# Head 3's attention probabilities through memory, with its scores and the products of heads 2 and 3 moved in TensorE's order

## The chip, the cores and the metric

One core of one Trainium2 chip. The metric is the device time of one execution in microseconds, the median of three runs. TensorE (PE) multiplies matrices, VectorE (DVE), ScalarE (ACT) and GpSimd (POOL) do elementwise work, and the sync engine (SP) issues nearly all the DMAs, in the order in which they are written. Each engine runs its instructions in order and waits on semaphores.

## The reference, cut to what matters

Tokens are 8 batches of 128, width 512. Two residual layers follow each other; the first one's attention is where the change lies: 32 heads of width 128, in 8 groups of 4.

```python
h_q = (rms(layernorm(x)) @ w_q.T)      # per head h
h_k, h_v = ctx @ w_k.T, ctx @ w_v.T
score = einsum('bqhd,bkhd->bhqk', h_q, h_k) + position_bias
score = where(mask, score, -inf); score = softmax(score, -1)
attn = einsum('bhqk,bkhd->bqhd', score, h_v)
x = x + tanh(g) * (hidden + attn @ w_out.T)
```

Behind it come a quantized feed-forward layer, a single-head attention and a layer of routed adapters, which the change does not touch.

## The kernel before, in words

The kernel is written out by hand: for each engine a list of calls, and the order of these lists is the order of the work. The groups of four heads are group 0 (`"first"`), groups 1 to 6 (`"loop"`, a loop on every engine) and group 7 (`"last"`). Float32 is split in a high and a low part; a product of two splits is three passes. In the loop the queries and keys of two heads come from seven products (`product`, Strassen's way, in the order `ORDER` = P1, P6, P2, P7, P5, P4, P3) whose right sides are blocks of x or of the context and combined blocks, fetched from memory into `ring` by SP (`fetch`, L407). Group 0 uses plain products (`plain`) and VectorE makes the combined blocks there (`combine_x`), which POOL splits (`combined_lo`) and SP stores (`put`, L404).

For each head, 8 batches at once:
- `scores` (TensorE, L1954) writes banks 4 and 5, four batches each. The second half waits until the head before has left bank 5.
- `softmax_in` (VectorE, L1374 and L1376) adds bias and mask (`bm`, made by POOL's `biasmask`, L682) and takes the maximum; `exps` (ScalarE, L952) does eight exponentials.
- `softmax_out` (VectorE), per half: a reciprocal (L1383), the multiplication into `turned_blocks` (L1396), and for heads 0 to 2 a transposition of 32x32 blocks (L1400).
- For heads 0 to 2 SP writes `turned_blocks` to memory (`passed`, L432) and reads it back so that whole blocks change places (`back`, four DMAs, L442) into `keyed`, the transposed probabilities. For head 3 (`h == TURNED`) VectorE writes them plainly (L1392), TensorE transposes them (`transposes`, L1982) and ScalarE copies them into `keyed` (`pt_out`, L939).
- `attend` (TensorE, L1970) multiplies values by `keyed` into banks 6 and 7; `ao_hi` (ScalarE, L958) and `ao_lo` (VectorE, L1405) split the result into `ao`.
- `project` (TensorE, L1998) makes 16 output tiles, 0 to 7 from heads 0 and 1 and 8 to 15 from heads 2 and 3, and `add_out` (VectorE, L1414) adds each to `acc`.

TensorE's order around the change, in a loop group: the seven products for heads 2 and 3 (the last is P3), scores of head 2, tiles 0 to 5, scores of head 3, tiles 6 and 7, two products, the product of head 2 with the values, three products, `transposes`, one product, head 3's product with the values, one product, tiles 8 to 15. SP's order there: write of head 2, a weight load (`v0`), return of head 2, a weight load (`q0`, L397), the bias (L446), then ring fetches and loads. In group 7 the products for the next group are replaced by `keys`, products of the second layer: their weights are loaded by SP into `raw_k`, scaled and split by ScalarE (`key_scaled`, L986, and `split_hi`, L998), which then copies two output weights (`vo_hi`, L906), all ahead of the exponentials of head 3. At the very start `warm` (L1841) runs matmuls on zeros.

Of the kernel before, what the change touches and what calls it, by code (L numbers as in the profile page):

```python
# [12 lines left out]
P = 128  # L13
# [79 lines left out]
def build(nc, a, out):  # L93
# [91 lines left out]

    TURNED = 3
# [64 lines left out]
    with ctx:  # L251
# [65 lines left out]

        s_pt, s_pte = s_cT, s_xT

# [72 lines left out]
        with nc.Block() as block:  # L392

            @block.sync
            def _(sp):
# [33 lines left out]
                def passed(g, h):  # L429

                    sp.wait_ge(s_turned, g * 2 * TURNED + 2 * h + 2)
# [3 lines left out]
                def back(g, m, h):  # L435
# [4 lines left out]
                    sp.wait_ge(s_passed, 16 * (g * TURNED + h) + 16)  # L440
# [47 lines left out]
                put(1, 3, 3)  # L488
                sp.wait_ge(s_bm, GH)
                bias_in(1)  # L490
                sp.wait_ge(s_plain, plain_at["q3b"])
# [14 lines left out]
                def body(g, m):  # L506
# [35 lines left out]
                    passed(g, 2)  # L542
                    sp.wait_ge(s_flo, 3 * prods(g, 3) + 3)
                    load(g + 1, "v0", 0)
                    back(g, m, 2)
# [3 lines left out]
                    bias_in(g + 1)  # L549
                    last_piece(prods(g, 3), 0)  # L550
# [10 lines left out]

                sp.wait_ge(s_prod, last_prod)
                sp.dma_start(raw_k[:, :, :], a["w_key"]).then_inc(s_raw["key"], 16)
                sp.wait_ge(s_spill, 32)
                sp.dma_start(raw_f[:, :, :], expanded).then_inc(s_raw["ffn"], 16)
                sp.dma_start(bkr[:, :], a["bk"].partition_broadcast(P)).then_inc(s_bk, 16)
                sp.dma_start(fnw[:, :], a["fnw"].partition_broadcast(P)).then_inc(s_fnw, 16)
                passed(LAST, 2)
                back(LAST, "last", 2)
                sp.wait_ge(s_vo_lo, vo_done(LAST, "last", "o3"))  # L570
                sp.dma_start(rows, a["rows"].partition_broadcast(P)).then_inc(s_rows, 16)
                sp.dma_start(wbm, a["w_bm"]).then_inc(s_bm1, 16)
                sp.wait_ge(s_tlo["key"], KC)
# [13 lines left out]
            def _(pool):  # L587
# [138 lines left out]
                combined_lo(1, 1, 3)  # L726
                vo_lo(0, "first", "o2")
                vo_lo(0, "first", "o3")
                plain_lo(9)
                biasmask(0, 3)  # L730
# [126 lines left out]
            def _(act):  # L857
# [75 lines left out]
                def pt_out(g):  # L933


                    act.wait_ge(s_pv, g * 2 * GH + 6)
                    for s in range(2):
                        act.wait_ge(s_pt, B + 2 * g + s + 1)
                        act.activation(keyed[:, :, :, :].rearrange("p i b q -> p (i b q)")[:, half(s)], bank[6 + s][:, :],  # L939
                                       ACT.Copy).then_inc(s_pte, 1)  # L940

# [128 lines left out]
                combined_hi(1, 2, 2, spare[:, :, :])  # L1070
                combined_hi(1, 3, 3)
# [13 lines left out]
                def body(g, m):  # L1085
# [38 lines left out]
                    if not last:  # L1124
                        first_out(g, m, 3)
                        vo_hi(g, "loop", "w0")
                        vo_hi(g, "loop", "w1")
# [1262 lines left out]
```

## Time and profile before

| What | us |
|---|---|
| median of 3 runs (lowest, highest) | 959.33 (958.12, 960.22) |
| the profiled execution | 959.01 |
| its span, first to last instruction | 957.2 |
| TensorE busy, matmuls | 941.9 (98%) |
| VectorE, ScalarE, POOL busy | 594.2, 399.5, 497.3 |
| mean rate of the DMAs | 208 GB/s |
| waits of TensorE for probabilities from memory | 5.6 |

How to read it: the groups take 97.4 us each (the first output tile of group 2 starts at 294.67, that of group 3 at 392.38), and the second layer starts near 821. Times of rows are microseconds from the start of the span, the mean of one instruction is in ns. The durations of matmuls overlap; their starts give the pace.

### The profile page before, as it was taken

Reading aid. Unit: us, or ns where it says so; the run is one execution under the profiler, and the core shown is the slowest. Engines: PE = TensorE matmul, PEld = TensorE weight load, DVE = VectorE, ACT = ScalarE, POOL = GpSimd, SP = SyncE. Lnnn points to the kernel's source line nnn. Section 1 sums busy time; section 2 is a strip of 40 time slices with the busy share of each in tenths; the row PEclk is TensorE's granted clock in tenths of the full one; section 3 lists DMA queues with packets and bytes.
Section 4 is the critical chain, followed back from the end, with each engine's and each line's share of the span. In section 5 each row is a group of like instructions: output and inputs, shape, how many; then the busy total and the mean of one; then the engine's idle time right before and its main releaser. Section 6 shows DMA issues by size and latency. Waiting matters only on the chain.

```text
span 957.2 us, 15391 instructions
## 1 busy us (share of the span) xinstructions
PE 941.9 (98%) x4850; PEld 793.9 (83%) x4850; DVE 594.2 (62%) x1020; ACT 399.5 (42%) x1080; POOL 497.3 (52%) x463
## 2 busy tenths in 40 slices
PE   9999899999999999999999999999999999999998
PEld 8888688788888888888888888888888888888885
DVE  4888846385538553855486447654666966756754
ACT  5765424252434233433443333433443346646630
POOL 3756754454446453646374637463646336687530
PEclk9999999999999999999999999999999999999999
DMA  7145676775687567766777667767687665200002
GB/s 283 45 152 222 234 255 249 259 266 196 241 276 275 219 241 263 271 244 241 251 271 256 241 241 260 270 248 237 226 292 266 230 224 183 91 23 1 2 1 88
DMA packets 67380, 199.44 MB, mean 208 GB/s; under 512 B 8720, under 2 KB 21264, under 8 KB 66320
## 3 DMA queue, kind: packets, MB, share of 16 engines
q1 hardware_dynamic: 66336, 197.67, 57.4%
q10 hardware_dynamic: 1008, 1.32, 0.4%
q8 instruction: 19, 0.31, 0.1%
q14 instruction: 17, 0.14, 0.0%
HBM read 174.85 MB, written 24.12 MB: 208 GB/s over the span
## 4 chain that ended last, share of the span: by engine, by line
PE 78%; DVE 8%; DMA 7%; issue 2%; SPq 2%; ACT 1%; POOL 1%; DVEq 0%; ACTq 0%
PE bank L1921 23%; PE bank L1998 16%; PE bank L2102 10%; PE bank L1937 10%; DMA keyed<-passing 6%; PE bank L1970 6%; PE bank L1954 5%; PE bank L1897 3%; PE bank L2126 2%; DVE turned_blocks L1396 1%; SPq L442 1%; DVE kt L1436 1%; DVE turned_blocks L1400 1%; PE bank L1982 1%; PE bank L2255 1%
## 5 line engine op out<-in xcount | busy, mean ns | idle before, releaser
L1998 PE MATMUL bank<-wvo,ao 128*128 128x512 f32 x768 | 179.9, 391 | 0.7 <-issue 0.6
L1937 PE MATMUL bank<-wvo,ct 128*128 128x512 f32 x768 | 177.7, 390 | 0.0
L1998 PEld LDWEIGHTS bank<-wvo,ao 128*128 128x128 f32 x768 | 143.0, 188 | 30.1 <-issue 1.0
L1937 PEld LDWEIGHTS bank<-wvo,ct 128*128 128x128 f32 x768 | 143.5, 188 | 29.3
L603 POOL TENSOR_TENSOR wvo<-stage,wvo 128x512 fp32r<-128x512 f32 x64 | 85.4, 1357 | 148.4 <-ACT wvo L906 148.3
L1921 PE MATMUL bank<-ring,wkq 128*128 128x512 f32 x648 | 157.4, 390 | 0.0
L1921 PEld LDWEIGHTS bank<-ring,wkq 128*128 128x128 f32 x648 | 121.2, 188 | 25.1
L1414 DVE SCALAR_TENSOR_TENSOR acc<-bank,gated_rows,acc 128x512 f32<-128x512 f32 x128 | 93.2, 742 | 39.4 <-PE bank L1998 38.3
L952 ACT ACTIVATE bank<-bank,nmax 128x128 f32<-128x128 f32 x256 | 88.2, 351 | 55.6 <-DVE nmax L1376 55.6
L1405 DVE TENSOR_TENSOR ao<-bank,ao 128x512 fp32r<-128x512 f32 x64 | 43.9, 691 | 106.6 <-ACT ao L958 106.6
L1436 DVE TENSOR_TENSOR qt<-bank,qt 128x512 f32<-128x512 f32 x98 | 66.4, 690 | 57.4 <-PE bank L1921 56.0
L682 POOL TENSOR_TENSOR bm<-maskneg,bias 128x1024 f32<-128x1024 f32 x32 | 78.9, 2465 | 26.0 <-DVE bank L1374 26.0
L945 ACT ACTIVATE vals<-bank 128x512 f32<-128x512 f32 x64 | 38.4, 600 | 94.7 <-PE bank L1937 94.4
L623 POOL TENSOR_TENSOR wkq_raw<-stage 128x256 f32<-128x256 f32 x27 | 20.3, 754 | 110.7 <-PE bank L1921 102.2
L1436 DVE TENSOR_TENSOR kt<-bank,kt 128x512 f32<-128x512 f32 x91 | 60.4, 682 | 26.6 <-PE bank L1921 25.0
L958 ACT ACTIVATE ao<-bank 128x512 fp32r<-128x512 f32 x64 | 37.9, 599 | 80.7 <-PE bank L1970 79.0
L1970 PEld LDWEIGHTS bank<-keyed,vals 128*128 128x128 f32 x512 | 61.0, 191 | 12.7 <-DMA keyed<-passing 11.1
L1970 PE MATMUL bank<-keyed,vals 128*128 128x128 f32 x512 | 63.6, 277 | 5.7 <-DMA keyed<-passing 5.6
L1374 DVE TENSOR_TENSOR bank<-bank,bm 128x512 f32<-128x512 f32 x64 | 44.4, 694 | 37.3 <-PE bank L1954 36.4
L1921 PE MATMUL bank<-xb,wkq 128*128 128x512 f32 x252 | 65.5, 395 | 0.0
L649 POOL TENSOR_TENSOR wkq<-wkq_raw,wkq 128x1024 fp32r<-128x1024 f32 x27 | 65.2, 2414 | 0.0
L1954 PEld LDWEIGHTS bank<-kt,qt 128*128 128x128 f32 x512 | 62.1, 191 | 3.4 <-DVE turned_blocks L1396 0.9
(187 smaller groups left out, 1511.9 us busy)
## 6 DMA issues: line engine op xcount, KB each, us to landing
ring<-combined SPq DMA_DIRECT2D x216, 512.0 KB, 6.3
stage<-in_w SPq DMA_DIRECT2D x63, 512.0 KB, 4.2
passing<-turned_blocks SPq DMA_DIRECT2D x24, 512.0 KB, 2.9
keyed<-passing SPq DMA_DIRECT2D x96, 128.0 KB, 3.2
combined<-work SPq DMA_DIRECT2D x16, 512.0 KB, 3.6
xraw<-in_x SPq DMA_DIRECT2D x2, 1024.0 KB, 11.3
bias<-in_bias SPq DMA_DIRECT2D x8, 256.0 KB, 4.5
cs<-in_ctx SPq DMA_DIRECT2D x1, 2048.0 KB, 7.8
```

The source lines that it names most:

```text
L603: pool.tensor_tensor(wvo[:, 1, h, :], stage[:, vo_stage(g, m, c)[0], :], wvo[:, 0, h, :].bitcast(fp32), ALU.subtract).then_inc(s_vo_lo, 1)
L649: pool.tensor_tensor(wkq[:, 3:7, 1, :, :].rearrange("p k c d -> p k (c d)"), wkq_raw[:, 3:7, 1, :, :].rearrange("p k c d -> p k (c d)"), w ...
L682: pool.tensor_tensor(bm[:, :, :], maskneg[:, :, :], bias[:, h:h + 1, :].to_broadcast([P, B, P]), ALU.add).then_inc(s_bm, 1)
L952: act.activation(scores, scores, ACT.Exp, bias=nmax[:, b:b + 1], accum_out=esum[:, b:b + 1]).then_inc(s_exp, 1)
L1414: dve.scalar_tensor_tensor(out=acc[:, b, :], in0=bank[un_of[m][f"o{i}"] % RING if to is None else to][:, :], scalar=gated_rows[:, b:b + 1] ...
L1436: dve.tensor_tensor(dst, bank[un_of[m][f"{ADDED[step]}.{j}"] % RING][:, :], other, ALU.add).then_inc(s_add, 1)
L1921: mm = pe.matmul(bank[b][:, :], wkq[:, FACTOR[p], w, c, :], right(s), start=(c == 0 and w + s == 0), stop=(c == 1 and w == 1))
L1937: mm = pe.matmul(bank[un_of[m][u] % RING][:, :], ct[:, i, c, b * P:(b + 1) * P], wvo[:, j, c, :], start=(c == 0 and i + j == 0), stop=(c = ...
L1954: mm = pe.matmul(bank[4 + s][:, (b - 4 * s) * P:(b - 4 * s + 1) * P], qt[:, h % 2, b * P:(b + 1) * P], kt[:, h % 2, b * P:(b + 1) * P], st ...
L1970: mm = pe.matmul(bank[6 + s][:, (b - 4 * s) * P:(b - 4 * s + 1) * P], vals[:, b, h * P:(h + 1) * P], right, start=True, stop=True)
L1998: mm = pe.matmul(bank[to][:, :], ao[:, h, p, b * P:(b + 1) * P], wvo[:, j, 2 * pair + h, :], start=(h == 0 and p + j == 0), stop=(h == 1 a ...
L2102: mm = pe.matmul(bank[b][:, 0:n], left(i, c), right[:, j, c, :], start=(c == 0 and i + j == 0), stop=(c == KC - 1 and i == 1 and last))
```

## The change

Head 3 takes the way of heads 0 to 2: `TURNED`, `transposes` and `pt_out` are gone, `softmax_out` turns blocks for every head, and `passed` and `back` are called for head 3. On TensorE the scores of head 3 stand behind three output tiles (before: six), the product of head 2 directly behind tile 7 and that of head 3 three products later (in group 7: one and two `keys` are moved). VectorE's, ScalarE's, POOL's and SP's lists follow: `softmax_in` and `softmax_out` of head 3 move forward between the additions; in SP's list the return of head 2 moves ahead of the `v0` load, the write of head 3 behind that load, and its return behind the `q0` load and the bias; in group 7 the write of head 2 moves ahead of the key weights' load. The diff, with context lines left out:

```diff
@@ -182,8 +182,6 @@
-    TURNED = 3
     R_FFN, R_BQ, R_BASE = range(3)
@@ -314,9 +312,6 @@
-        s_pt, s_pte = s_cT, s_xT
@@ -428,7 +423,7 @@
-        sp.wait_ge(s_turned, g * 2 * TURNED + 2 * h + 2)
+        sp.wait_ge(s_turned, g * 2 * GH + 2 * h + 2)
         sp.dma_start(passing[h % 2, :, :, :, :].rearrange("i k j c -> (i k) j c"),
@@ -437,7 +432,7 @@
             sp.wait_ge(s_pv, g * 2 * GH + 2 * h)
-        sp.wait_ge(s_passed, 16 * (g * TURNED + h) + 16)
+        sp.wait_ge(s_passed, 16 * (g * GH + h) + 16)
         for j in range(4):
@@ -485,9 +480,11 @@
     put(1, 2, 2)
-    put(1, 3, 3)
     sp.wait_ge(s_bm, GH)
     bias_in(1)
+    passed(0, 3)
+    put(1, 3, 3)
+    back(0, "first", 3)
     sp.wait_ge(s_plain, plain_at["q3b"])
@@ -540,13 +537,15 @@
         passed(g, 2)
+        back(g, m, 2)
         sp.wait_ge(s_flo, 3 * prods(g, 3) + 3)
         load(g + 1, "v0", 0)
-        back(g, m, 2)
+        passed(g, 3)
         sp.wait_ge(s_vo_lo, vo_done(g, "loop", "o3"))
         bias_in(g + 1)
+        back(g, m, 3)
         last_piece(prods(g, 3), 0)
@@ -559,17 +558,19 @@
+    passed(LAST, 2)
     sp.wait_ge(s_prod, last_prod)
     sp.dma_start(raw_k[:, :, :], a["w_key"]).then_inc(s_raw["key"], 16)
+    back(LAST, "last", 2)
     sp.wait_ge(s_spill, 32)
     sp.dma_start(bkr[:, :], a["bk"].partition_broadcast(P)).then_inc(s_bk, 16)
+    passed(LAST, 3)
     sp.dma_start(fnw[:, :], a["fnw"].partition_broadcast(P)).then_inc(s_fnw, 16)
-    passed(LAST, 2)
-    back(LAST, "last", 2)
     sp.wait_ge(s_vo_lo, vo_done(LAST, "last", "o3"))
     sp.dma_start(wbm, a["w_bm"]).then_inc(s_bm1, 16)
+    back(LAST, "last", 3)
     sp.wait_ge(s_tlo["key"], KC)
@@ -724,10 +725,10 @@
     combined_lo(1, 1, 3)
+    biasmask(0, 3)
     vo_lo(0, "first", "o2")
     plain_lo(9)
-    biasmask(0, 3)
@@ -929,15 +930,6 @@
-    def pt_out(g):
-        act.wait_ge(s_pv, g * 2 * GH + 6)
-        for s in range(2):
-            act.wait_ge(s_pt, B + 2 * g + s + 1)
-            act.activation(keyed[:, :, :, :].rearrange("p i b q -> p (i b q)")[:, half(s)], bank[6 + s][:, :],
-                           ACT.Copy).then_inc(s_pte, 1)
@@ -1068,14 +1060,13 @@
     combined_hi(1, 2, 2, spare[:, :, :])
+    exps(0, 3, range(2))
     combined_hi(1, 3, 3)
-    exps(0, 3, range(2))
     vo_hi(0, "first", "w0")
     plain_out("k4b")
-    pt_out(0)
     plain_out("k5a")
@@ -1121,15 +1112,14 @@
         exps(g, 3, range(2))
+        ao_hi(g, 2)
         if not last:
             vo_hi(g, "loop", "w1")
-        ao_hi(g, 2)
         if last:
                 split_hi("ffn", c)
-        pt_out(g)
         ao_hi(g, 3)
@@ -1381,18 +1371,10 @@
         dve.reciprocal(rinv[:, bs], esum[:, bs]).then_inc(s_rinv, 1)
-        if h and s == 0:
-            dve.wait_ge(s_passed, 16 * (g * TURNED + h))
-        elif s == 0 and m != "first":
-            dve.wait_ge(s_pt, B + 2 * g)
+        if s == 0 and (m, h) != ("first", 0):
+            dve.wait_ge(s_passed, 16 * (g * GH + h))
         dve.wait_ge(s_rinv, n + 1)
-        if h == TURNED:
-            dve.tensor_tensor(turned_blocks[:, :, :, :].rearrange("p j b k -> p (j b k)")[:, half(s)].rearrange("p (b k) -> p b k", b=4),
-                              bank[4 + s][:, :].rearrange("p (b k) -> p b k", b=4),
-                              rinv[:, bs].unsqueeze(2).to_broadcast([P, 4, P]), ALU.mult).then_inc(s_p, 1)
-            return
         dve.tensor_tensor(turned_blocks[:, :, bs, :].rearrange("p j b k -> p b j k"),
@@ -1657,17 +1639,17 @@
     softmax_out(0, "first", 2, 1)
+    softmax_in(0, 3)
     add_out(0, "first", 3)
     add_out(0, "first", 4)
+    softmax_out(0, "first", 3, 0)
+    add_out(0, "first", 5)
     combine_x([8])
-    add_out(0, "first", 5)
+    softmax_out(0, "first", 3, 1)
+    add_out(0, "first", 6)
     combine_x([9])
-    softmax_in(0, 3)
-    add_out(0, "first", 6)
     add_out(0, "first", 7)
-    softmax_out(0, "first", 3, 0)
-    softmax_out(0, "first", 3, 1)
     ao_lo(0, 2)
@@ -1703,28 +1685,26 @@
         add_out(g, m, 1)
+        softmax_out(g, m, 2, 1)
         add_out(g, m, 2)
-        softmax_out(g, m, 2, 1)
+        softmax_in(g, 3)
         add_out(g, m, 3)
+        softmax_out(g, m, 3, 0)
         add_out(g, m, 4)
+        softmax_out(g, m, 3, 1)
         add_out(g, m, 5)
-        softmax_in(g, 3)
         add_out(g, m, 6)
         add_out(g, m, 7)
-        softmax_out(g, m, 3, 0)
-        softmax_out(g, m, 3, 1)
+        ao_lo(g, 2)
         if last:
             key(0)
-            ao_lo(g, 2)
             key(1)
+            ao_lo(g, 3)
             key(2)
+        else:
+            sums(g, m, 3, ("u2", "C11"))
             ao_lo(g, 3)
-        else:
-            sums(g, m, 3, ("u2",))
-            ao_lo(g, 2)
-            sums(g, m, 3, ("C11", "u3", "C22", "u4", "C21"))
-            ao_lo(g, 3)
-            sums(g, m, 3, ("C12",))
+            sums(g, m, 3, ("u3", "C22", "u4", "C21", "C12"))
             for i in range(B, 2 * B):
@@ -1956,32 +1936,15 @@
     def attend(g, h):
-        if h < TURNED:
-            pe.wait_ge(s_keyed, 64 * (g * TURNED + h) + 64)
+        pe.wait_ge(s_keyed, 64 * (g * GH + h) + 64)
         for s in range(2):
                 pe.wait_ge(s_val_out, 8 * g + 4 * s + 4)
-            if h == TURNED:
-                pe.wait_ge(s_pte, B + 2 * g + s + 1)
-            else:
-                pe.wait_ge(s_aolo, g * 2 * GH + 2 * h + s + 1)
+            pe.wait_ge(s_aolo, g * 2 * GH + 2 * h + s + 1)
             for b in range(4 * s, 4 * s + 4):
-                right = keyed[:, :, b, :] if h < TURNED else keyed[:, :, :, :].rearrange("p i b q -> p (i b q)")[:, b * P:b * P + P]
                 mm = pe.matmul(bank[6 + s][:, (b - 4 * s) * P:(b - 4 * s + 1) * P],
-                               vals[:, b, h * P:(h + 1) * P], right, start=True, stop=True)
+                               vals[:, b, h * P:(h + 1) * P], keyed[:, :, b, :], start=True, stop=True)
             mm.then_inc(s_pv, 1)
-    def transposes(g):
-        n = g * 2 * GH + 2 * TURNED
-        for s in range(2):
-            pe.wait_ge(s_p, n + s + 1)
-            pe.wait_ge(s_aolo, n + s + 1)
-            for b in range(4 * s, 4 * s + 4):
-                mm = pe.transpose(bank[6 + s][:, (b - 4 * s) * P:(b - 4 * s + 1) * P],
-                                  turned_blocks[:, :, :, :].rearrange("p j b k -> p (j b k)")[:, b * P:b * P + P], ident[:, :])
-            mm.then_inc(s_pt, 1)
@@ -2030,15 +1993,14 @@
     scores(0, "first", 2)
-    for i in range(6):
+    for i in range(3):
         project(0, "first", i)
     scores(0, "first", 3)
-    project(0, "first", 6)
-    project(0, "first", 7)
+    for i in range(3, B):
+        project(0, "first", i)
     plain("k4a")
     plain("k4b")
-    transposes(0)
     plain("k5a")
@@ -2068,30 +2030,25 @@
         scores(g, m, 2)
-        for i in range(6):
+        for i in range(3):
             project(g, m, i)
         scores(g, m, 3)
-        project(g, m, 6)
-        project(g, m, 7)
+        for i in range(3, B):
+            project(g, m, i)
+        attend(g, 2)
         if last:
             keys(0)
-            attend(g, 2)
             keys(1)
-            transposes(g)
+            attend(g, 3)
             keys(2)
-            attend(g, 3)
             for i in range(B, 2 * B):
             return
-        product(g, m, 3, "P1")
-        product(g, m, 3, "P6")
-        attend(g, 2)
-        for p in ORDER[2:5]:
+        for p in ORDER[:3]:
             product(g, m, 3, p)
-        transposes(g)
-        product(g, m, 3, "P4")
         attend(g, 3)
-        product(g, m, 3, "P3")
+        for p in ORDER[3:]:
+            product(g, m, 3, p)
         for i in range(B, 2 * B):
```

## Rows read from the trace of the kernel before

**Rows 1.** The page, busy time, share of the span and instructions of TensorE
```profile
PE 941.9 (98%) x4850; PEld 793.9 (83%) x4850; DVE 594.2 (62%) x1020; ACT 399.5 (42%) x1080; POOL 497.3 (52%) x463
```

**Rows 2.** Groups by line, TensorE; busy us, mean ns, then idle before
```profile
L1982 PE MATMUL bank<-ident,turned_blocks 128*128 128x128 f32 x64 | 8.5, 274 | 2.3 <-DVE ao L1405 2.3
```

**Rows 3.** The chain that ended last, group 2; start us, us, what
```profile
294.67 8.20 PE bank L1998 x36
302.87 1.78 PE bank L1954 x16
...
310.10 1.78 PE bank L1970 x16
...
316.03 0.87 PE bank L1982 x8
...
318.28 1.78 PE bank L1970 x16
...
321.46 10.88 PE bank L1998 x48
```

**Rows 4.** Timeline of VectorE, group 2; start us, us, what
```profile
298.84 1.37 DVE L1414 SCALAR_TENSOR_TENSOR acc<-bank,gated_rows,acc 128x512 f32<-128x512 f32 x2
300.13 0.17 DVE L1383 RECIPROCAL rinv<-esum 128x4 f32<-128x4 f32 x1
...
301.05 0.71 DVE L1400 STREAM_TRANSPOSE turned_blocks<-turned_blocks 128x512 f32<-128x512 f32 x1
...
303.86 0.70 DVE L1374 TENSOR_TENSOR bank<-bank,bm 128x512 f32<-128x512 f32 x1
...
306.53 1.64 DVE L1414 SCALAR_TENSOR_TENSOR acc<-bank,gated_rows,acc 128x512 f32<-128x512 f32 x2
```

**Rows 5.** Timeline of ScalarE, group 2, the last exponential of head 3
```profile
307.74 0.37 ACT L952 ACTIVATE bank<-bank,nmax 128x128 f32<-128x128 f32 x1
```

**Rows 6.** Timeline of SP's queue, group 2; start and time of the issues
```profile
301.79 0.32 SPq L432 DMA_DIRECT2D passing<-turned_blocks  x1
...
304.65 1.74 SPq L442 DMA_DIRECT2D keyed<-passing  x4
306.65 0.36 SPq L397 DMA_DIRECT2D stage<-in_w  x1
307.30 0.36 SPq L446 DMA_DIRECT2D bias<-in_bias  x1
```

**Rows 7.** Waits of TensorE in the whole run; us, times, longest
```profile
PE bank L1970 <- DMA keyed<-passing: 5.6, 9, 1.7
```

**Rows 8.** The chain that ended last, head 0's return in group 2
```profile
271.02 8.41 DMA keyed<-passing
```

**Rows 9.** Timeline of SP's queue, group 0
```profile
101.63 0.32 SPq L432 DMA_DIRECT2D passing<-turned_blocks  x1
...
111.15 3.19 SPq L404 DMA_DIRECT2D combined<-work  x4
```

**Rows 10.** Timeline of TensorE, group 0, the product of head 2
```profile
108.69 2.05 PE L1970 MATMUL bank<-keyed,vals 128*128 128x128 f32 x16 [1.14 <-DMA keyed<-passing]
```

**Rows 11.** The chain that ended last, output tile 8 of group 0
```profile
124.34 10.88 PE bank L1998 x48
```

**Rows 12.** The DMA view, the load of the key weights; us to landing last
```profile
raw_k<-in_w_key SPq DMA_DIRECT2D x1, 1024.0 KB, 4.8
```

**Rows 13.** Timeline of ScalarE, group 7
```profile
787.46 2.59 ACT L986 ACTIVATE raw_k<-raw_k,fncol 128x512 f32<-128x512 f32 x4
...
792.00 1.17 ACT L906 ACTIVATE wvo<-stage 128x512 fp32r<-128x512 f32 x2
```

**Rows 14.** The chain that ended last, output tiles of group 7
```profile
784.03 8.20 PE bank L1998 x36
...
810.25 11.18 PE bank L1998 x48
```

**Rows 15.** Timeline of TensorE at the start, matmuls on zeros
```profile
1.05 4.44 PE L1841 MATMUL bank<-qt 128*128 128x128 f32 x20 [1.05 <-DVE qt L1306]
```

## The prediction

> **What bounds the kernel now.** Read the page first. TensorE is busy for 941.9 of 957.2 us [rows 1], so what the change does is decided by what TensorE executes and by what it waits for. The profiled execution took 959.01 us, 1.8 us more than its span and 0.3 us under the median 959.33; every sum below is made against 959.0. The second view is the chain of waits in one group of heads (group 2; groups 1 and 3 to 6 repeat it): from the end of head 2's scores at 294.67 to output tile 8 at 321.46 it is TensorE without a gap [rows 3]. I call 294.67 zero: output tiles cost 1.37 each (8.20 for 6), a head's scores or its product with the values 1.78, a product of seven 1.37 as well, the eight transposes 0.87, and tile 8 begins at 26.8. The third is what feeds it: VectorE's and ScalarE's softmax [rows 4, 5] and SP's queue [rows 6]. The waits list says that heads 0 to 2, which already go through memory, are late nine times, 5.6 us in all [rows 7]: that trip has almost no slack.
>
> **What is removed.** `transposes` (64 matmuls) and `pt_out` go. The group view gives them 274 ns each [rows 2], but they overlap: in the chain eight take 0.87 [rows 3], so 7.0 us in eight groups, plus the 2.3 us wait of group 0 [rows 2]. The Trainium skill, "TensorE: Matmul & The Clock Gate", Part 4: PE-mode transpose, gives about 275 ns for a transpose in a kernel; by that eight would be worth 2.2 us and the whole removal 17.6. The chain's spacing decides, and I take 7.0. `pt_out`'s two copies on ScalarE hide beside TensorE, and their going gives nothing.
>
> **What is added, in a loop group.** First VectorE. Now it ends head 2's second half at 301.05 + 0.71, that is +7.1 [rows 4]. One addition (0.65, half of 1.29) moves behind it, so it ends at +6.45, and `passed` for head 2 is issued then. The scores of head 3 come three tiles after zero, at +4.1. Their first half (0.89) ends at +5.0, but the second needs bank 5, freed by the multiplication that ends at +5.75: TensorE waits 0.75. This isn't added to the sum, because a later wait covers it. Next VectorE adds tile 2 (+7.1) and does `softmax_in(3)`: 306.53 - 303.86 = 2.67, to +9.75. POOL's `biasmask` needs only head 2's scores read and keeps its place, so it is in time. Tile 3 is added (+10.4). The exponentials end 308.11 - 303.86 = 4.25 after `softmax_in` began [rows 4, 5], at +11.35, so they cost nothing. Then two `softmax_out` of 1.63 each (300.13 to 301.76) with one addition between: head 3's turned probabilities are ready at **+14.3**.
>
> Now the trip through memory. SP is free (head 2's return was issued near +9.3, the load of v0 after it). For head 2 now the write is issued at 301.79, the returns from 304.65, and the product starts at 310.10 without a wait: at most 8.3 us [rows 6, 3]. In group 0, with no load between write and return, the product waited for it and began at 108.69 after the issue at 101.63: 7.06 us [rows 9, 10]. For head 3 the q load (512 KB) and the bias (256 KB), which now stand behind head 2's return [rows 6], fall between write and return. Head 2's trip carries one load of 512 KB there; I take its 8.3 plus 0.5 for the other 256 KB: 8.8. Ends: 7.06, and, if the queues are as full as behind head 0, 2.9 for the write, 1.3 to the last issue and 8.41 after it [rows 6, 8] = 12.6. So head 3's product starts at **+23.1**. TensorE's own work brings it there at 8 x 1.37 + 1.78 + 0.75 + 1.78 + 3 x 1.37 = +19.4 (a little later if head 2's return is late), so it waits near 3.7 us. Behind the product (2.05 when it was waited for [rows 10]) come four products, 5.5: tile 8 at +30.65 against +26.8. That is **3.8 us slower** per group. In six groups 22.8; waits for head 2 that this absorbs are part of the 5.6 us [rows 7], and I give a third back, 1.8: **+21.0**. The ring fetches behind `back` 3 go out at about +19; the first to be used, for P4, is wanted at +28. Next group's weights need the last products, whose distance to the next group is unchanged. Both cost nothing while a landing stays under 9 us.
>
> **Group 0.** Here VectorE also makes the combined blocks. `softmax_in(3)` (2.67) and both `softmax_out` (3.3) move ahead of step 9 of `combine_x`, so POOL's lower part, and with it the stores that SP issued at 111.15 [rows 9], come about 6 us later, 117.1. In SP's queue `passed` for head 3 stands behind one such store and the bias: some 1.5 later, 118.6. Another 1 MB store stands between it and the return. The trip is 9.2 by my choice (7.06 to 12.6): product at 127.8, then 2.05 and one unit of 2.73: tile 8 at 132.6 against 124.34 [rows 11]: **+8.3**, with the transposes' waits already inside.
>
> **Group 7.** `passed` for head 2 moves ahead of the 1 MB key weights in SP's queue. They are issued now before 784.03; then near 784.03 + 6.45 + 0.4 = 790.9. The landing takes 4.8 [rows 12] and one more for the write before it: 796.7. On ScalarE the scaling and splitting of these weights and two weight copies, 793.17 - 787.46 = 5.7 [rows 13], stand ahead of head 3's exponentials, so these start at 802.4 and end at 805.2 (eight in 2.8). The second `softmax_out`, behind an addition, ends at 807.8. SP then issues head 3's write, and rows, norm weights and adapters (1.3 MB) lie between it and the return: trip 9.6, product at 817.4. With keys(2), 2.77, tile 8 comes at 822.2 against 810.25 [rows 14]: **+12.0**.
>
> **The clock.** The granted clock is 1.00 (2.4 GHz) in every stretch, and no wait behind the first scores exceeds 2.3 us. At the start 20 matmuls took 4.44 us, 0.22 each [rows 15], where the transposes take 0.11 [rows 3]: half the pace, as at 1.2 GHz, though the column doesn't show it. What a wait of 6 to 9 us does, this trace doesn't show: at least 0, at most that start again, 2.2 lost each time. Groups 0 and 7 get three such waits, 0 to 6.6; I take two, **4.4**, because the one idle engine that the trace shows, at the start, was slow. The same page of the Trainium skill, Part 1: The HAM clock gate, says that an idle TensorE is set to half its clock; by that rule all three would cost.
>
> **Sum**: 959.0 + 21.0 + 8.3 + 12.0 + 4.4 = 1004.7, so 1005. With trips of 7.06 everywhere and no clock loss: 6 x 1.74 + 2.1 + 2.5 less, 985. With 12.6 everywhere and 6.6 of clock: 22.8 + 3.4 + 3.0 + 2.2 more, 1036.
>
> **Rivals.** (a) The trips are short, as in group 0: 985 to 993. For it, the v0 load no longer stands inside head 2's trip; against, the bias and q loads do inside head 3's. (b) The queues are fuller than for head 2: from 1020 to 1036. For it, head 0's return took 8.41 after its last issue [rows 8]; against, eight ring fetches stood ahead of that one, and here only three transfers. (c) TensorE falls to half its clock after the loop's waits of 3.7 us too: six more times 2.2, that is 1018. For it, they are longer than the 2.3 seen; against, the products on both sides are dense. (d) **Faster.** The return lands before TensorE asks: this needs a trip under 19.4 - 14.3 = 5.1 us in the loop. Then 7.0 are gained and, with the late returns and the 2.3, up to 9 more goes: 950. Against it is the shortest trip seen, 7.06, two microseconds above the point. (e) In group 7 the order of the key weights' load doesn't hold up head 3, since they land early enough: then that group costs 3.8 and the sum is 996. Against, ScalarE runs its instructions in order.
>
> **Numbers.** Chances: forecast (993 to 1013) 0.55, (a) 0.15, (b) 0.12, (c) 0.07, (d) 0.03, (e) 0.08. The range 985 to 1022 holds forecast, (a), (c), (e) and the near end of (b), and leaves out (d) and most of (b). About 0.2%, 2 us, is what a measurement of this kernel can tell from no change. Faster only in (d): 0.03; same 0.01; slower 0.96.
>
> **What would show it.** In the profile after: waits of TensorE's line of the head products for the return from memory, some 3.7 us in each of six groups and more in groups 0 and 7, some 40 us in all; the write of head 3 issued 14.3 after the end of head 2's scores; a wait of 0.75 in the scores of head 3; key weights issued near 6.9 after that zero in group 7 instead of before it; the matmul after a long wait at twice its spacing. The forecast is wrong if the product of head 3 starts within 19.4 of zero, or if VectorE is ready much before 14.3.

## The result, and the profile after

The changed kernel takes 1018.55 us (median of 4 runs, 1016.99 to 1022.18), the kernel before, run beside it, 958.73 (957.88 to 960.22): a ratio of 1.0621, 95% interval 1.0599 to 1.0644. It is 60 us slower (59.8 by the medians, 59.5 by the ratio). The forecast was 1005 with a range of 985 to 1022: sign and range hold, the size was 13.5 too small. The profiled execution took 1017.53, its span is 1015.7, 58.5 more than before.

The page of the kernel after: busy time, and the granted clock in 40 slices (tenths).

```profile
PE 954.0 (94%) x4786; PEld 801.2 (79%) x4786; DVE 601.1 (59%) x1036; ACT 390.5 (38%) x1064; POOL 494.8 (49%) x463
PEclk9999989999999999999999999999989997999999
```

TensorE has 64 instructions fewer and is busy 12.1 us **longer** than in [rows 1]. Work was taken away and the time of the rest grew: mostly matmuls at a lower clock, as the windows below show. The other 46 us are idle time. The waits of TensorE (total, times, longest):

```profile
PE bank L1945 <- DMA keyed<-passing: 41.1, 17, 9.5
PE bank L1934 <- DVE turned_blocks L1378: 10.7, 9, 3.2
PE bank L2059 <- DVE acc L1396: 3.6, 1, 3.6
```

L1945 is `attend`, L1934 `scores`, L1961 `project`, L2059 the second layer's `keys` (L1970, L1954 and L1998 before, for the first three). The wait for probabilities from memory, 5.6 in [rows 7], is now 41.1.

**A loop group.** The chain of group 2, as in [rows 3]; start, time, what:

```profile
313.80 4.13 PE bank L1961 x18
...
328.04 2.97 DMA passing<-turned_blocks
...
336.08 2.05 PE bank L1945 x16
338.13 5.48 PE bank L1901 x24
343.61 10.88 PE bank L1961 x48
```

Zero, the end of head 2's scores, is 313.80. Tile 8 starts at +29.81 where [rows 3] have +26.79. (Before, a loop group takes 97.9 in the mean: five lie between 294.67 and 784.03, [rows 3, 14]; the 97.4 stated ahead is a little low.) The part between is no longer TensorE's: head 3's probabilities are written at +14.24 and its product starts at +22.28. SP's queue there, and TensorE's timeline (in brackets the idle time before, and who ended it), the latter with head 3's product in groups 2, 4, 5 and 6:

```profile
320.27 0.32 SPq L427 DMA_DIRECT2D passing<-turned_blocks  x1
...
324.91 0.36 SPq L392 DMA_DIRECT2D stage<-in_w  x1
328.04 0.34 SPq L427 DMA_DIRECT2D passing<-turned_blocks  x1
328.63 0.34 SPq L392 DMA_DIRECT2D stage<-in_w  x1
329.23 0.45 SPq L441 DMA_DIRECT2D bias<-in_bias  x1
331.03 1.75 SPq L437 DMA_DIRECT2D keyed<-passing  x4
```

```profile
319.55 1.16 PE L1934 MATMUL bank<-kt,qt 128*128 128x128 f32 x8 [0.75 <-DVE turned_blocks L1378]
...
336.08 2.05 PE L1945 MATMUL bank<-keyed,vals 128*128 128x128 f32 x16 [2.58 <-DMA keyed<-passing]
...
538.25 2.60 PE L1945 MATMUL bank<-keyed,vals 128*128 128x128 f32 x16 [2.71 <-DMA keyed<-passing]
...
640.41 2.05 PE L1945 MATMUL bank<-keyed,vals 128*128 128x128 f32 x16 [2.96 <-DMA keyed<-passing]
...
742.02 3.78 PE L1945 MATMUL bank<-keyed,vals 128*128 128x128 f32 x16 [3.27 <-DMA keyed<-passing]
```

The same 16 matmuls take 2.05 at 336 and 640 and 3.78 at 742, behind waits of nearly the same length. The stretches by clock (start to end, busy times, granted clock, DMA) show why:

```profile
336.08:340.00 3.92, 3.92 (x25) 3.58 (x26) 1.82 (x3) 1.19 (x2) 0.39 (x1) 1.00 0.81 301
538.20:543.00 4.80, 4.75 (x22) 4.27 (x23) 1.38 (x2) 1.19 (x2) 0.00 (x0) 0.64 0.64 246
742.00:750.00 8.00, 7.98 (x31) 7.13 (x32) 2.50 (x4) 1.19 (x2) 1.13 (x2) 0.64 0.41 144
861.00:866.00 5.00, 4.46 (x19) 4.27 (x20) 0.70 (x2) 1.24 (x3) 0.00 (x0) 0.50 0.17 69
```

0.50 is 1.2 GHz, half of the 2.4 that the column showed in every stretch before; a figure between is a stretch that holds both. It fell behind the loop's wait in groups 1, 4 and 6, not in 2, 3 and 5.

From zero to tile 8, groups 1 to 6 took 27.40, 26.79, 26.79, 27.07, 27.09, 27.27 before and take 31.97, 29.81, 29.83, 31.51, 30.19, 33.22: together **+24.1**.

**Group 7.** The chain, and under it ScalarE's wait for the key weights and SP's queue:

```profile
830.37 6.23 DMA raw_k<-in_w_key
...
847.64 3.14 DMA passing<-turned_blocks
...
852.66 8.84 DMA keyed<-passing
861.54 3.78 PE bank L1945 x16
...
869.05 10.90 PE bank L1961 x48
```

```profile
836.62 2.56 ACT L978 ACTIVATE raw_k<-raw_k,fncol 128x512 f32<-128x512 f32 x4 [9.51 <-DMA raw_k<-in_w_key]
```

```profile
834.90 0.43 SPq L566 DMA_DIRECT2D raw_f<-expanded  x1
...
847.64 0.32 SPq L427 DMA_DIRECT2D passing<-turned_blocks  x1
848.01 1.24 SPq L569 DMA_DIRECT2D fnw<-in_fnw  x1
...
849.79 0.43 SPq L572 DMA_DIRECT2D stage<-in_w_bm  x1
850.85 2.38 SPq L437 DMA_DIRECT2D keyed<-passing  x4
```

From zero (823.54) to tile 8 it is 45.5 against 26.2 in [rows 14]: **+19.3**. From the write's issue to the product are 13.9 us.

**Group 0.** Its chain:

```profile
120.30 6.70 DMA passing<-turned_blocks
128.38 3.33 DMA keyed<-passing
131.75 3.78 PE bank L1945 x16
...
138.92 10.88 PE bank L1961 x48
```

Tile 8 starts 14.6 later than in [rows 11], of which 0.9 is there at the group's start already. The write, issued in one run with two blocks' stores, landed after 6.7. Sum: 14.6 + 24.1 + 19.3, and 0.5 in the rest of the span, is the 58.5.

### The profile page after: what moved, and what is told of

It is laid out like the page before. It is cut to its first block, busy times and chain, and to the rows that moved or that the text cites. A ratio compares the mean times of both kernels' runs of the same rounds, so it can differ in the third digit from the quotient of the medians.

```text
span 1015.7 us, 15271 instructions
## 1 busy us (share of the span) xinstructions
PE 954.0 (94%) x4786; PEld 801.2 (79%) x4786; DVE 601.1 (59%) x1036; ACT 390.5 (38%) x1064; POOL 494.8 (49%) x463
## 4 chain that ended last, share of the span: by engine, by line
PE 66%; DMA 13%; DVE 12%; issue 3%; SPq 2%; ACT 2%; POOL 1%; DVEq 0%; ACTq 0%; POOLq 0%
PE bank L1901 20%; PE bank L1961 12%; PE bank L1917 9%; PE bank L2059 9%; DMA keyed<-passing 9%; PE bank L1945 5%; PE bank L1934 4%; DVE turned_blocks L1378 3%; DMA passing<-turned_blocks 3%; PE bank L1877 3%; SPq L437 2%; DVE acc L1396 2%; PE bank L2083 2%; DVE turned_blocks L1382 2%; ACT bank L944 1%
## 5 line engine op out<-in xcount | busy, mean ns | idle before, releaser
L1961 PE MATMUL bank<-wvo,ao 128*128 128x512 f32 x768 | 180.6, 393 | 0.0
L1961 PEld LDWEIGHTS bank<-wvo,ao 128*128 128x128 f32 x768 | 143.7, 189 | 29.5
L1945 PE MATMUL bank<-keyed,vals 128*128 128x128 f32 x512 | 72.8, 302 | 41.1 <-DMA keyed<-passing 41.1
L1945 PEld LDWEIGHTS bank<-keyed,vals 128*128 128x128 f32 x512 | 68.2, 212 | 50.2 <-DMA keyed<-passing 30.4
L1934 PE MATMUL bank<-kt,qt 128*128 128x128 f32 x512 | 65.4, 279 | 10.7 <-DVE turned_blocks L1378 10.7
L1934 PEld LDWEIGHTS bank<-kt,qt 128*128 128x128 f32 x512 | 63.4, 193 | 15.1 <-DVE turned_blocks L1378 10.0
```

Source lines behind the costliest of these rows:

```text
L1934: mm = pe.matmul(bank[4 + s][:, (b - 4 * s) * P:(b - 4 * s + 1) * P], qt[:, h % 2, b * P:(b + 1) * P], kt[:, h % 2, b * P:(b + 1) * P], st ...
L1945: mm = pe.matmul(bank[6 + s][:, (b - 4 * s) * P:(b - 4 * s + 1) * P], vals[:, b, h * P:(h + 1) * P], keyed[:, :, b, :], start=True, stop=True)
L1961: mm = pe.matmul(bank[to][:, :], ao[:, h, p, b * P:(b + 1) * P], wvo[:, j, 2 * pair + h, :], start=(h == 0 and p + j == 0), stop=(h == 1 a ...
```

## The experiments

Two questions: how much of the excess is the clock and how much the trips, and is it the way through memory or the new places that cost 60 us? "After" below is 1018.55. Kernels of one batch share their runs of the kernel before, medians 960.88 (e1 to e4), 960.11 (e5 to e8) and 959.36 (e9 and e8 again). Differences to after are those of the medians; by the ratios e2 is 10 less instead of 8, and the others come out within 1.5.

### e1: the waits filled with matmuls (from the kernel after)

```diff
+    def filler(n):
+        for _ in range(n):
+            pe.matmul(bank[6][:, 0:P], vals[:, 0, 0:P], vals[:, 0, 0:P], start=True, stop=True)
-    attend(g, 3)
+    attend(g, 3, 9)
```

`attend` calls `filler` with that number (two matmuls' records each) ahead of its wait: 9 in the loop, 44 in group 0, 32 in group 7 and 8 there for head 2; 8 and 13 stand ahead of the halves of head 3's scores in group 0. These matmuls are added work whose results nobody reads.

> The kernel after, with matmuls whose result nobody reads put in TensorE's waits: 8 and 13 calls before the two halves of head 3's scores in group 0, 44 before head 3's product there, 9 before it in each loop group, 8 before head 2's and 32 before head 3's product in group 7 (0.22 us each, about as long as the waits that the profile after shows). Theory A, the clock: after its waits TensorE runs at half pace for a stretch, which costs about 15.6 us by the profile after (groups 0: 4.2, 1: 1.4, 4: 1.6, 6: 2.7, 7: 5.7); with the waits filled the granted clock stays at 1.00, save near the wait for keys in group 7 that stays unfilled, and the time falls by 9 to 14 us, to 1005 to 1010, although TensorE does more work. Theory B, the slow product after the wait is the DMAs' traffic in the memory that TensorE reads: then it stays slow, and the time is the same or up to 3 us longer where a filler outlasts its wait.

Measured: 1005.67 (1003.79 to 1013.25, 4 runs), ratio 1.0495 (1.0438 to 1.0553), mean clock 0.995 instead of 0.976. Group 0, timeline of TensorE:

```profile
120.01 9.98 PE L1942 MATMUL bank<-vals 128*128 128x128 f32 x88
129.84 1.95 PE L1954 MATMUL bank<-keyed,vals 128*128 128x128 f32 x16
```

The product behind 10 us of unread work takes 1.95; behind 9.5 us of waiting it took 3.78, so theory B is out. Nothing else was changed, TensorE executes 318 instructions more (5104 to 4786), and the kernel is 13 us faster by the medians. So **about 13 us of the 60 are the clock**; the size is rough, for the two ratio intervals leave 6 to 18, and the profiled executions differ by 11. It isn't quite all of the clock: behind a wait of 2.07 that the filler left in group 5, the product still takes 3.68. What remains, 45 over its own runs of the kernel before, is the forecast's sum without its clock term (41.3) plus 4.

### e2: group 7, key weights ahead of head 2's write (from after)

```diff
-    passed(LAST, 2)
     sp.wait_ge(s_prod, last_prod)
     sp.dma_start(raw_k[:, :, :], a["w_key"]).then_inc(s_raw["key"], 16)
+    passed(LAST, 2)
     back(LAST, "last", 2)
```

> The kernel after with one part undone: in group 7 the load of the key weights stands ahead of head 2's write in SP's queue again. Theory A: 13.6 of the 19.3 us lost in group 7 (the rest is clock) come from ScalarE, whose scaling of these weights stands ahead of head 3's exponentials; with the load first, the exponentials start near 9.2 instead of 18.7 us after head 2's scores, head 3's product 9 us earlier and the time falls by 9 to 15 us. Theory B: the return of head 3, which waits behind 1.3 MB of rows, norm weights and adapters, is what is late whatever ScalarE does (its trip took 13.9 us), and those loads follow later weights: less than 5 us.

Measured: 1010.47 (1006.87 to 1014.32, 4 runs), ratio 1.0520 (1.0471 to 1.0570): 8 less than after by the medians and 10 by the ratios, so at or just under the low end of the 9 to 15 that theory A expected. SP's queue and the product:

```profile
843.26 0.32 SPq L427 DMA_DIRECT2D passing<-turned_blocks  x1
...
848.68 1.90 SPq L437 DMA_DIRECT2D keyed<-passing  x4
```

```profile
858.31 3.72 PE L1945 MATMUL bank<-keyed,vals 128*128 128x128 f32 x16 [8.41 <-DMA keyed<-passing]
```

Head 3's write now goes out 14.5 after zero (828.76), as in a loop group, instead of 24.1: the step "ScalarE's work on the key weights stands ahead of the exponentials" is confirmed. But the trip became longer, 15.05 instead of 13.9, and ate a part of it.

### e3: in the loop, head 3's return ahead of the q load and the bias (from after)

```diff
     passed(g, 3)
+    back(g, m, 3)
     sp.wait_ge(s_vo_lo, vo_done(g, "loop", "o3"))
     load(g + 1, "q0", 1)
     ...
     bias_in(g + 1)
-    back(g, m, 3)
```

> The kernel after, with the q load and the bias behind head 3's return in SP's queue of the loop groups. Theory A (my term of contention): the trip of 8.0 to 8.75 us becomes the 7.1 of group 0's head 2, head 3's product comes 0.9 to 1.6 us earlier in six groups, and the time falls by 6 to 12 us (clock losses shrink too). Theory B: the trip is the two fixed latencies and the four issues, the loads between don't lengthen it: under 1 us in all.

Measured: 1004.65 (1001.99 to 1005.67, 4 runs), ratio 1.0465 (1.0429 to 1.0501): 14 less, more than the 6 to 12 of theory A; theory B is out. In group 2 the write is issued at 325.86, the return at 328.56, 2.7 behind it (3.0 in the kernel after), and the product starts at 333.27, 7.4 behind the write instead of 8.0. Over the six groups the trips take 7.1 to 7.6, and 8.3 in group 1, instead of 8.0 to 8.75. The six waits are 2.65, 1.80, 1.01, 2.14, 1.99 and 1.41 instead of 2.94, 2.58, 2.02, 2.71, 2.96 and 3.27: 5.5 less. The other 8 to 9 go with the shorter waits: no product behind them is at half pace now (2.05 in all six groups), and the mean clock is 0.985 instead of 0.976. That last share is worked out, not isolated.

### e4: head 3's product three products later (from after)

```diff
-    for p in ORDER[:3]:
+    for p in ORDER[:6]:
         product(g, m, 3, p)
     attend(g, 3)
-    for p in ORDER[3:]:
-        product(g, m, 3, p)
+    product(g, m, 3, "P3")
```

> The kernel after, with head 3's product in the loop groups three products later, directly ahead of the last one (P3), VectorE's list to match. Theory A (distance): TensorE arrives 23.5 us after head 2's scores, where the data are there at 22.3 to 23.0; the waits for head 3 and the half pace behind them go in groups 1 to 6, which then take 26.7 us to tile 8 instead of 29.8 to 33.2: 24 to 28 us less, 991 to 995. Theory B: the ring's fetches and weights behind the return become the next wait, and half or less of it is gained.

Measured: 1002.22 (998.27 to 1006.32, 4 runs), ratio 1.0457 (1.0419 to 1.0496): 16 less, not 24 to 28. The wait for head 3 is gone in the loop, and another stands in its place. Waits of TensorE, and the chain in group 3:

```profile
PE bank L1945 <- DMA keyed<-passing: 20.4, 8, 9.7
...
PE bank L1901 <- DMA ring<-combined: 7.7, 6, 2.0
```

```profile
422.82 3.07 DMA passing<-turned_blocks
...
427.80 6.00 DMA ring<-combined
...
434.80 1.78 PE bank L1945 x16
```

The ring piece for P4 is fetched behind head 3's return in SP's queue, and the return waits for the write. SP stands still with it, and everything behind it goes out late. The mechanism of theory B, that the next late piece takes over, holds; its size ("half or less") was too low, for 16 of 24 to 28 were gained. The six waits for the ring, 0.3 to 2.0 each, are 7.7 of what is missing.

### e5: the way through memory alone, the orders of before (from before)

```diff
     bias_in(g + 1)
+    passed(g, 3)
     last_piece(prods(g, 3), 0)
+    back(g, m, 3)
-            transposes(g)
-    pt_out(g)
```

In group 0 write and return of head 3 stand behind the bias, in group 7 around the loads of norm weights, rows and adapters. TensorE's order is that of before, but for one place that the text below passes over: in group 7 head 3's product takes the place of the transposes, ahead of `keys(2)`, where before it stood behind it. So it is asked for one `keys` (2.77) earlier there. In the same group head 2's write and return also stay ahead of the norm weights' load, as in the change.

> Head 3 through memory as in the change, but nothing else moved: the lists of TensorE, VectorE and ScalarE and the loads in SP's queue stand as before, and head 3's write and return are put in where their data come. Theory A: the trip itself doesn't fit. Its data are ready 16.7 us after head 2's scores, come back at 25, and TensorE asks at 22.7: a wait of 2.3 us in each loop group, some 5 in group 0 and 9 in group 7; with some clock loss 985 to 992, so about half of the change's loss is the trip and the other half the places that its parts were moved to. Theory B: without the earlier scores it is worse than the change: over 1018.

Measured: 989.40 (988.39 to 994.76, 4 runs), ratio 1.0324 (1.0283 to 1.0365). So the trip costs some 30 us about where head 3 stood before (up to 2.8 of it by the place in group 7), and **the other moves of the diff add another 29**. Its waits for probabilities are 33.6 in all, 9.2 for head 3 in group 0 and 10.3 in group 7, and 0.5 to 2.6 in the loops. The one in group 7:

```profile
833.48 3.78 PE L1947 MATMUL bank<-keyed,vals 128*128 128x128 f32 x16 [10.33 <-DMA keyed<-passing]
```

### e6: other places in the loop (from after)

```diff
-    for i in range(3):            # output tiles ahead of scores(g, m, 3)
+    for i in range(4):
-    for p in ORDER[:3]:           # products ahead of attend(g, 3)
+    for p in ORDER[:5]:
     passed(g, 3)
+    back(g, m, 3)
+    last_piece(prods(g, 3), 0)    # fetch for P4, both ahead of q0 and the bias
```

> The kernel after with other places in the loop groups alone: head 3's scores after four output tiles (frees the 0.74 us wait for bank 5), its product after five products, its return and the fetch of the ring piece for P4 ahead of the q load and the bias. Theory A (distance and queue): no waits for head 3 and for the ring, 27.0 us from head 2's scores to tile 8 in groups 1 to 6 as before the change, so 24 us less than the change: 992 to 997. Theory B (the ring's piece for P4, late by 0.3 to 2.0 us where head 3's product stood behind six products, stays late): 998 to 1003.

Measured: 990.82 (989.20 to 993.31, 4 runs), ratio 1.0332 (1.0302 to 1.0362): 28 less than after, better than expected. No wait for the ring and none for head 3 is left in the loops, and from zero to tile 8 it is 27.0 to 27.9. What is left there is a wait of 0.8 to 1.7 for head 2's return in each group. e3 shortened the waits and e4 exchanged them for others; the order of the queue and the distance together (a product two places later, P4's fetch and one tile moved as well) do what neither did alone.

### e7: group 7, loads behind head 3's return too (from e2)

```diff
     passed(LAST, 3)
+    back(LAST, "last", 3)
     sp.dma_start(fnw[:, :], a["fnw"].partition_broadcast(P)).then_inc(s_fnw, 16)
     ...
     sp.dma_start(wbm, a["w_bm"]).then_inc(s_bm1, 16)
-    back(LAST, "last", 3)
```

> The kernel after with SP's queue of group 7 changed alone: the key weights' load first, as in the run before, and norm weights, rows and adapters (1.3 MB) behind head 3's return. With the load first alone, head 3's trip took 15.1 us in the profile (write 5.4, return 9.6) against 8.0 to 8.8 in the loop. Theory A, those loads: the trip falls to about 10 us, head 3's product comes 4 to 5 us earlier than with the load first alone, 1004 to 1008. Theory B, the 1 MB of feed-forward weights and the bias row issued before the write fill the queues: the trip stays over 13 us, 1009 to 1012.

Measured: 1005.66 (1004.86 to 1009.41, 4 runs), ratio 1.0490 (1.0456 to 1.0524): 13 less than after, and 3 less than e2 by the ratios, 5 by the medians. The intervals of e7 and e2 overlap, so the times alone don't tell the two apart; the trip does. SP's queue and the product:

```profile
836.87 0.43 SPq L566 DMA_DIRECT2D raw_f<-expanded  x1
...
840.43 0.32 SPq L427 DMA_DIRECT2D passing<-turned_blocks  x1
845.95 1.74 SPq L437 DMA_DIRECT2D keyed<-passing  x4
847.73 0.43 SPq L570 DMA_DIRECT2D fnw<-in_fnw  x1
```

```profile
850.40 3.18 PE L1945 MATMUL bank<-keyed,vals 128*128 128x128 f32 x16 [3.36 <-DMA keyed<-passing]
```

With the three loads out of the way the return takes 4.45 from its first issue instead of 9.6, and the trip 10.0 instead of 15.05. So **the loads between write and return cost group 7 5 us** (one trace each). The write still needs 5.5, behind a 1 MB load (`raw_f`) issued 3.6 earlier.

### e8 and e9: every place moved

e8 takes the places of e6 and e7, puts head 2's product behind P1, head 3's product of group 7 behind all three `keys`, and reorders group 0. e9 moves further what e8 still waited for: ScalarE's `ao_hi` and exponentials of head 3 forward, the combined blocks of group 0 behind them, VectorE's additions of tiles 3 and 4 ahead, a weight load (`v2`) for group 1 ahead of seven ring fetches, the `raw_f` load behind head 3's return.

```diff
@@ e8, TensorE, group 0, ahead of the scores of head 3
-    for i in range(3):
+    for i in range(6):
@@ e8, TensorE, loop
-    attend(g, 2)
+    product(g, m, 3, "P1")
+    attend(g, 2)
@@ e9, SP, group 7
-    sp.dma_start(raw_f[:, :, :], expanded).then_inc(s_raw["ffn"], 16)
     sp.dma_start(bkr[:, :], a["bk"].partition_broadcast(P)).then_inc(s_bk, 16)
     passed(LAST, 3)
     back(LAST, "last", 3)
+    sp.dma_start(raw_f[:, :, :], expanded).then_inc(s_raw["ffn"], 16)
@@ e9, ScalarE, group 7
+    ao_hi(g, 3)
     ...
         split_hi("ffn", c)
-    ao_hi(g, 3)
@@ e9, ScalarE, group 0
-    combined_hi(1, 2, 2, spare[:, :, :])
     exps(0, 3, range(2))
+    combined_hi(1, 2, 2, spare[:, :, :])
```

> All parts together, to see whether the change can win: the loop groups as in the run with other places, and head 2's product behind P1; group 7 with the quiet queue and head 3's product behind all three key products; group 0 with head 3's scores after six tiles, head 2's second half ahead of combine step 6, head 3's write and return ahead of the stores, and both products two units later. If distance and queue are all, the loop groups take 26.0 to 26.8 us, group 0 ends 0 to 2 us earlier than before the change and group 7 up to 3 us later: 955 to 963, no clear difference from the kernel before. If each wait taken away uncovers another, 975 or more.

Measured: 961.63 (958.92 to 965.16, 10 runs) beside 960.11 (13 runs), ratio 1.0023 (1.0005 to 1.0041), as expected if distance and queue are all. From zero to tile 8 the loop groups take 26.2 to 26.9, group 0 ends 1.4 earlier than in [rows 11] and group 7 takes 1.9 longer than in [rows 14]. Left are waits of 3.4 for VectorE at tile 7 of group 0, of 2.0 for ScalarE in the first loop group and of 1.7 for the return in group 7; e9 goes after these.

> The version with all places, once more, with what its own profile shows late: in group 0 output tile 7 waits 3.4 us for VectorE's addition of tile 3 (the additions of tiles 3 and 4 go ahead of head 3's softmax and combine step 6, the exponentials of head 3 ahead of the high part of that step), and group 1 waits 2.0 us for a load that stands behind seven ring fetches (it goes ahead of them); in group 7 the 1 MB of feed-forward weights go behind head 3's return (its write took 5.3 us to land behind them), their split behind head 3's. If these waits are what is left, 6 to 8 us less than the version before it and 0.2 to 0.8% under the kernel before the change: 952 to 957. If the gain is taken by the next late step, 958 to 962, the same as before the change.

> The version with all places as it was, on the same chip and in the same rounds as the next one: 958 to 963, within 0.4% of the kernel before.

Measured: e9 960.92 (957.19 to 965.08, 12 runs) beside 959.36 (23 runs), ratio 1.0009 (0.9991 to 1.0026); e8 in the same batch 964.17 (959.49 to 968.10, 10 runs), ratio 1.0049 (1.0030 to 1.0067), a little over what was expected. For e9 the second expectation came true, the gain taken by the next late step, and not 952 to 957. e9's waits of TensorE:

```profile
PE bank L1946 <- DMA keyed<-passing: 5.9, 9, 1.7
PE bank L1902 <- DMA ring<-combined: 4.0, 1, 4.0
PE bank L2086 <- ACT xnr L1148: 1.4, 1, 1.4
```

On its page TensorE is busy for 937.8 us, 4.1 less than in [rows 1], and its span is 958.0, 0.8 more. So the 60 us can be had back with the trip in place, to within what is measured here, and no version that beats the kernel before was found. What is gained, later pieces take. Group 0 ends 4.1 earlier than in [rows 11] and the loop groups are faster by 3.7 from zero to tile 8; but 6.2 are lost between tile 8 of group 0 and the end of head 2's scores in group 1, a ring fetch 4.0 late among them, and 1.4 behind group 7, where ScalarE feeds a transposition for the second layer late. Whether the order that avoids these two would beat the kernel before was not tried. Nor was the kernel before with those of e9's moves that don't need the trip (the `v2` load, for one), so how much of the 60 came back by the trip's own places is not shown.

## Why the prediction was right, and where it was short

- **What is removed, 7.0.** e9, where the transposes are gone too and the clock is 9 tenths or more in every slice (0.998 in the mean), shows TensorE 4.1 less busy than before: that suggests that 7.0 is high rather than low, and 17.6 is out of the question. The 275 ns of the Trainium skill ("TensorE: Matmul & The Clock Gate", Part 4: PE-mode transpose) for one transpose agrees with the mean of [rows 2], 274, but instructions overlap, and the chain's 0.11 each is the price in time.
- **What would show it.** The waits for the return were put at some 40 in all, and are 41.1; the key weights' issue in group 7 at +6.9, and it is at +6.8.
- **Loop: the way to +14.3.** Held to a tenth: the write is issued at +14.24. The wait of 0.75 for bank 5 was there, 0.74 or 0.75 in each loop group and group 7, and as forecast it costs nothing of its own.
- **Loop: the trip, 8.8.** Measured 8.0 to 8.75. A little too long, so the waits were 2.0 to 3.3, not 3.7. Rivals (a) and (d) fell: no trip of the loop was near 7.06. Rival (b), fuller queues, was wrong here and right in groups 0 and 7. Without the clock the six groups lost 18.0 (24.1 less 6.1), against 21.0.
- **Group 0, +8.3; measured +13.7** beside the 0.9 of its start. The write goes out at 120.30, 1.7 later than the forecast 118.6 (0.9 of that is the later start), its trip takes 11.45 instead of 9.2, inside the bounds 7.06 to 12.6 but nearer to the other end, and from the product to tile 8 it takes 7.2 instead of 4.8, which is the clock. Waits of 2.28 and 3.24 for VectorE in head 3's scores (the 3.2 of the list above) were not forecast. The second of them and the half pace behind it lie on the chain to the write: in e1, where they are filled, the write goes out 1.4 earlier (118.89), 0.5 of it ahead of these scores already.
- **Group 7, +12.0; measured +19.3.** Each instant up to the write came as worked out: issue at +24.1 for +23.8. Rival (e) fell with it, and e2 shows its mechanism. **The trip is the mis-sized term: 9.6 in the forecast, 13.9 measured**, over my upper bound of 12.6. I had put 1.3 on head 2's 8.3 for the 1.3 MB of norm weights, rows and adapters, a rate that no row supported; e7 beside e2 shows them to cost 5. The clock adds 2.7.
- **The clock, 4.4: the other mis-sized term.** On the path it is 11.5: half of the slow time in group 0 (2.6), group 7 (2.8) and loop groups 1, 4 and 6 (6.1, from windows such as 742 to 750, 8.0 x 0.36 = 2.9). Slow stretches ahead of a long wait add little: behind group 7's first two waits nothing (in e1 the write goes out no sooner after zero), behind group 0's scores up to 0.9, which these 11.5 leave out. e1 measured 13 by an experiment, give or take 6. The step that failed is "groups 0 and 7 get three such waits": the loop's waits brought it too, in three groups of six. That is rival (c), half true; it had asked for all six. Part 1 of the same page of the Trainium skill, The HAM clock gate, says that an idle TensorE is set to half its clock; the 0.50 of the rows agrees as to the level, and the groups at full clock behind 2.6 and 2.96 us of waiting show that the trace must tell when.

The time lies outside the 993 to 1013 of the forecast proper and on the 1018 of rival (c), but not by (c) alone: of what was missing some 7 are the clock and some 6 the rest, which is 9 too few in groups 0 and 7 and around them, less 3 too many in the loop. So errors of both signs stand behind the total. Rival (d)'s 950 doesn't follow from its own terms (959 less 7 and less up to 9 is 943); nothing rests on it.

The balance: 41.3 without the clock was forecast and 47 measured (+4.3 for the trip of group 7, +2.3 for that of group 0, +1.1 for the issues of the two writes, +1.4 for group 0's start and the rest of the span, -3.0 in the loop); the clock was 4.4 and is 11.5 by the stretches, 13 by e1.

## What to carry to other kernels

A round trip through memory costs latency, not work: place it where the consumer has independent work for as long as the trip takes (here 8 to 9 us for 512 KB) between write and use, and keep loads out of its queue from ahead of the write until the return is issued. Count a new wait of TensorE twice, as idle time and as the half clock that may follow, and tell the two apart with unread matmuls in the wait (e1). Moving one late piece shows the next one behind it in the same queue (e4), so judge places together (e6).

## What the runs showed of the hardware that was not expected

- **The price of the same round trip.** 512 KB out and back took 7.06 with little beside it [rows 9, 10], 7.1 to 7.6 in e3 and once 8.3, 8.0 to 8.75 with 768 KB between write and return, 10.0 in e7, 11.45 among stores in group 0, 13.9 and 15.05 with over 1 MB of loads between. Against the 7.06, more than half of the 15.05 goes with other transfers around it: 5 with those between (e7), and part with those issued ahead of the write, for in e9, with `raw_f` out of the way, the write of group 7 lands after 3.7 instead of e8's 5.3.
- **Half pace after short waits, but not always.** Waits of 2.7 to 3.3 us were followed by 1.2 GHz in groups 1, 4 and 6, waits of 2.0 to 3.0 in groups 2, 3 and 5 were not. With the same orders in the loop, the product behind was slowed in five groups of six in e7 (waits of 2.44 to 3.32) and in five of six in e2, where a wait of 2.97 passed at full clock. The wait's length alone doesn't decide; what else does stays open, and a comparison of two single traces can hold a few microseconds of it.
- **More work, less time.** 318 instructions added in the waits made the kernel about 13 us faster.
